# Cross attention and a 4-bit FFN on one core: the dequantisation is spread over the setup and the projections of the first chunk, with two pairs of PSUM banks

## The reference

```python
# cross attention: 16 heads, dk = 8, 4 superposed states
qh, kh, vh = (interfere(proj(t, W, b)) for ...)      # t = LN(x), ctx, ctx
# interfere(y) = y + 0.1 * amp * einsum('bhsdi,hij->bhsdj', y, interference)
scores = einsum('bhqdm,bhkdm->bhqkm', qh, kh) / sqrt(8)
x = x + (softmax(scores, over keys) applied to vh) @ Wo.T + bo
# FFN with 4-bit weights, 512 -> 2 x 1376 -> 512
W[i, j] = sc[g[i], j] * (wq[i, j] - (zq[g[i], j] + 1))
gate, up = split(LN(x) @ W_gu);  x = x + (silu(gate) * up) @ W_d
```

## Time and profile before

| | |
|---|---|
| median of three runs | 906.57 us |
| profiled execution | 906.32 us, its span 904.6 us |
| mean granted TensorE clock | 0.90 |
| PE busy | 772.6 us, 85% of the span |
| DVE busy | 510.2 us, 56% |
| ACT busy | 438.3 us, 48% |
| POOL busy | 326.8 us, 36% |
| chain that ended last | PE 67%, DVE 15%, ACT 8%, issue 6%, DMA 2% |

### The profile page before, as it was taken

The page is one execution under the profiler, slowest core; times in us unless marked ns, Lnnn a source line. Parts: engine busy times, 40 slices in busy tenths (PEclk is TensorE's granted clock), DMA queues, the critical chain, the costliest instruction groups (busy, mean ns, idle before and its releaser), DMA issues.

```text
span 904.6 us, 23874 instructions
## 1 busy us (share of the span) xinstructions
PE 772.6 (85%) x9953; PEld 562.3 (62%) x9953; DVE 510.2 (56%) x1013; ACT 438.3 (48%) x806; POOL 326.8 (36%) x290
## 2 busy tenths in 40 slices
PE   5306457766799999999999999999999999999898
PEld 5303323322278857876787778677857885787484
DVE  6987745554465646655574556456645663644421
ACT  1426355676365526662555455454635462655120
POOL 6732324555314530543064114412431352144220
PEclk9758655565599999999999999999999999999999
DMA  8900113222101011002100110011001100010000
GB/s 248 292 23 1 50 32 89 69 56 63 32 25 28 3 49 50 3 3 71 28 2 14 60 28 3 13 60 28 2 21 52 28 2 25 3 27 3 24 1 23
DMA packets 20702, 36.98 MB, mean 41 GB/s; under 512 B 3374, under 2 KB 7602, under 8 KB 20592
## 3 DMA queue, kind: packets, MB, share of 16 engines
q1 hardware_dynamic: 20604, 35.48, 13.5%
HBM read 26.56 MB, written 4.19 MB: 34 GB/s over the span
## 4 chain that ended last, share of the span: by engine, by line
PE 67%; DVE 15%; ACT 8%; issue 6%; DMA 2%; SPq 1%; DVEq 0%; ACTq 0%; POOL 0%
PE bank L511 16%; PE bank L526 13%; PE bank L482 9%; PE bank L492 9%; PE bank L644 4%; DVE nmf L1166 4%; PE bank L638 3%; PE bank L661 3%; ACT arena L849 3%; PE bank L619 2%; PE bank L459 2%; DVE arena L1094 2%; DMA arena<-in_L_xattn_Wo 2%; DVE arena L985 2%; PE bank L443 2%
## 5 line engine op out<-in xcount | busy, mean ns | idle before, releaser
L511 PE MATMUL bank<-arena,WGU 128*128 128x256 f16 (+1 forms) x2112 | 247.0, 274 | 1.4 <-DVE arena L709 1.4
L511 PEld LDWEIGHTS bank<-arena,WGU 128*128 128x128 f16 (+1 forms) x2112 | 206.2, 100 | 27.5 <-DVE arena L709 1.6
L1368 POOL TENSOR_TENSOR arena<-arena 128x512 f16<-128x512 f32 x128 | 147.0, 1173 | 190.5 <-ACT arena L856 190.5
L482 PE MATMUL bank<-arena,WT 128*128 128x256 f16 x768 | 91.3, 281 | 40.4 <-DVE arena L709 39.1
L526 PE MATMUL bank<-WD,arena 128*128 128x512 f16 (+1 forms) x528 | 121.1, 379 | 0.0
L849 ACT ACTIVATE arena<-bank,small 128x512 f32<-128x512 f32 x128 | 89.1, 776 | 58.3 <-PE bank L644 58.3
L1355 POOL TENSOR_TENSOR arena<-arena 128x512 f16<-128x512 f32 (+1 forms) x48 | 51.7, 1077 | 172.2 <-ACT arena L829 172.2
L482 PEld LDWEIGHTS bank<-arena,WT 128*128 128x128 f16 x768 | 76.9, 101 | 54.6 <-issue 43.1
L492 PE MATMUL bank<-WT,arena 128*128 128x512 f16 x384 | 88.0, 387 | 1.8 <-DVE arena L707 1.8
L526 PEld LDWEIGHTS bank<-WD,arena 128*128 128x128 f16 (+1 forms) x528 | 49.4, 98 | 53.2
L1166 DVE TENSOR_REDUCE nmf<-bank 128x8 f32<-128x512 f32 x128 | 79.4, 682 | 4.4 <-PE bank L619 4.2
(11 more groups left out here) (157 smaller groups left out, 1068.8 us busy)
## 6 DMA issues: line engine op xcount, KB each, us to landing
arena<-in_L_ffn_qweight_gu SPq DMA_DIRECT2D x8, 688.0 KB, 5.4
arena<-arena SPq DMA_DIRECT2D x32, 144.0 KB, 3.0
WT<-in_ctx SPq DMA_DIRECT2D x8, 512.0 KB, 15.1
arena<-in_ctx SPq DMA_DIRECT2D x8, 512.0 KB, 3.7
arena<-in_x SPq DMA_DIRECT2D x8, 512.0 KB, 3.6
out_y<-arena SPq DMA_DIRECT2D x16, 256.0 KB, 2.1
arena<-in_L_ffn_qweight_down SPq DMA_DIRECT2D x10, 256.0 KB, 3.4
arena<-in_L_xattn_Wk SPq DMA_DIRECT2D x1, 1024.0 KB, 6.6
```

The lines of the kernel that those rows point to most:

```text
L482: mm = e.matmul(jb[:, g2 * TOK:(g2 + 1) * TOK], WT[:, w, sp, kb, g * P:(g + 1) * P], src[:, mp, kb, :], start=(n == 0), stop=(n == 11))
L511: mm = e.matmul(pb[0:m, i * TOK:(i + 1) * TOK], WGU[:, sp, kb, half * INTER + fb * P:half * INTER + fb * P + m], x2T[:, mp, kb, :], start= ...
L1368: e.tensor_tensor(phl[:, a, 1, :], pring[:, a, :], phl[:, a, 0, :], ALU.subtract).then_inc(S["p_lo"], 1)
```

## The change

- **The ticks.** There are 40 now, from the ctx maxima on. Three stand in the setup (after the 4th, 6th and 8th ctx maximum), three after the scales, two after each of the first two weights' halves, five behind the first key operations and five behind the value rows; slots 0 and 1 have one each, every batch four, and the tail two. The steps of a tick are further apart: on TensorE unit n - 2, on VectorE the integers of n and the product of n - 3, on ScalarE the conversion of n first, then the scaled difference of n - 2 and the high half of n - 4, on POOL the remainder of n - 5.
- **The banks.** Units below 17 alternate between two pairs, the second being JB[0] and JB[1]. From unit 17 on there is the one pair, as before. The folds have the four AB banks for all weights.
- **The tables.** The gate/up scales are split in three parts on VectorE in a layout over 128 partitions, the zero points in one over 32, and 12 and 4 transfers bring them into the row layout. The one-hot matrix of gate/up is made on VectorE. The quantisation scales have an all-reduce of their own. The down tables stay on POOL and ScalarE.
- **The rest.** The 32 copies that permute Wo are on ScalarE. The quantised weights are loaded earlier. The transposed ctx is made ahead of the ticks of w0.

The diff, cut to its core:

```diff
-TICKS = ND + 3
-FIRST_SLOT = 2
-TICK_ENDS = [0] * FIRST_SLOT + [TICKS * (k + 1) // (SLICES - FIRST_SLOT) for k in range(SLICES - FIRST_SLOT)]
...
+TICKS = ND + 5
+PLACES = ["ctx4", "ctx6", "ctx8", "scales", "w0", "w1", "keys", "values"] + list(range(SLICES))
+TICKS_AT = {"ctx4": 1, "ctx6": 1, "ctx8": 1, "scales": 3, "w0": 2, "w1": 2, "keys": 5, "values": 5}
+BATCH_TICKS = [0, 1] + [slot[j] for slot in IN_BATCH for j in (0, 2, 3, 3)] + AT_TAIL[:2]
+assert sum(TICKS_AT.values()) + len(BATCH_TICKS) == TICKS
+TICKS_AT.update((k, BATCH_TICKS.count(k)) for k in BATCH_TICKS)
+TWO_PAIRS = sum(TICKS_AT[p] for p in PLACES[:PLACES.index("values") + 1]) - 3
+def ticks(place):
+    before = sum(TICKS_AT.get(p, 0) for p in PLACES[:PLACES.index(place)])
+    return range(before, before + TICKS_AT.get(place, 0))
 
...
+            load_w(e, 1)
+            e.dma_start(scw, sc_gu.rearrange("g (r n) -> (g r) n", r=32)).then_inc(S["scw_loaded"], 16)
+            e.dma_start(zraww[0:32, :], qz_gu.rearrange("g (r n) -> (g r) n", r=8)).then_inc(S["zw_loaded"], 16)
...
-                e.dma_start(scgu[32 * i:32 * i + GROUPS_GU, :], sc_gu).then_inc(S["sc_loaded"], 16)
                 e.dma_start(scd[32 * i:32 * i + GROUPS_D, :], sc_d).then_inc(S["sc_loaded"], 16)
-            for c in range(NCHUNK):
-                e.dma_start(cmax_st[:, c].rearrange("p (t n) -> p t n", t=TILES), c_d[c]).then_inc(S[f"ctxm_loaded{c}"], 16)
+            e.dma_start(gidx_d[0:96, :].bitcast(I32), gi_d.partition_broadcast(96)).then_inc(S["gid_loaded"], 16)
+            load_w(e, 2)
+            e.dma_start(gidx_gu[0:96, :].bitcast(I32), gi_gu.partition_broadcast(96)).then_inc(S["gi_loaded"], 16)
+            load_w(e, 0), load_w(e, 3)
+            for c in range(4):
+                load_ctx_max(e, c)
+            load_piece(e, 0)
+            e.wait_ge(S["sc_zeroed"], 2)
+            e.wait_ge(S["wide_ready"], 1)
+            for i in range(PARTS):
+                for g in range(GROUPS_GU):
+                    e.dma_start(sc3_gu[32 * i + g:32 * i + g + 1, :], sc3w[32 * g:32 * g + 32, i, :]).then_inc(S["sc_table"], 16)
+            e.wait_ge(S["zwide_ready"], 1)
+            for g in range(GROUPS_GU):
+                e.dma_start(z_gu[g:g + 1, :], zw[8 * g:8 * g + 8, :]).then_inc(S["z_table"], 16)
+            for c in range(4, NCHUNK):
+                load_ctx_max(e, c)
             e.dma_start(cin, c_d[0]).then_inc(S["ctx_loaded"], 16)
             e.dma_start(xin, x_d[0]).then_inc(S["x_loaded"], 16)
-            load_piece(e, 0)
             load_piece(e, 1)
             e.dma_start(bo_row[:, :], bo.partition_broadcast(P)).then_inc(S["bo_loaded"], 16)
+            for i in range(2, 6):
+                load_next_piece(e, i)
...
-                banks = bank[4 * (i % 2):4 * (i % 2) + 4]
                 e.wait_ge(S[f"w_loaded{w}"], 16)
...
+                if i:
+                    e.wait_ge(S["fold_evicted"], i)
+                else:
                     e.wait_ge(S["bias_evicted"], 1)
...
-                            mm = e.matmul(banks[cb][:, g * P:(g + 1) * P], wraw[w][:, g, cb * P:(cb + 1) * P],
...
+            for place in ("ctx4", "ctx6", "ctx8", "scales"):
+                pe_ticks(e, place)
+            e.wait_ge(S["fold_evicted"], 4)
+            for t in range(TILES):
+                pe_transpose_tile(e, -1, f"cT{t}", cin, S["ctx_loaded"], 16)
+            pe_ticks(e, "w0")
+            pe_ticks(e, "w1")
+        def pe_ticks(e, place):
+            for n in ticks(place):
+                pe_dequant(e, n - 2)
+        def dq_banks(n):
+            return (JB[0], JB[1]) if n < TWO_PAIRS and n % 2 == 0 else (GB, UB)
...
+            reached(e, S["d_w"], n - 1 if n < TWO_PAIRS else n)
+            e.matmul(scale[0:m, 0:cols], hot[0:64 + groups, pick], sc3[0:64 + groups, c0:c0 + cols], start=True, stop=True)
...
             if first:
+                pe_ticks(e, "keys")
                 e.wait_ge(S["wlo_done"], 2)
...
+                pe_ticks(e, "values")
...
                 e.wait_ge(S["wlo_done"], 3)
                 e.wait_ge(S["t_lo"], t_at(-1, "xT1"))
+                e.wait_ge(S["d_w"], TWO_PAIRS)
...
         def act_setup(e):
+            for i in range(2):
+                act_scale_part(e, i)
...
             for i, w in enumerate(WORDER):
+                if w == 3:
+                    act_permute(e)
...
-                    ins = e.activation(wraw[w][:, cb], bank[4 * (i % 2) + cb][:, :], ACT.Copy)
+                    ins = e.activation(wraw[w][:, cb], AB[cb][:, :], ACT.Copy)
...
+            act_scale_part(e, 2)
+            for place in ("ctx4", "ctx6", "ctx8", "scales"):
+                act_ticks(e, place)
             e.wait_ge(S["scale_ready"], 1)
             act_whi(e, 0)
             act_hi(e, -1, "cT0"), act_hi(e, -1, "cT1")
+            act_ticks(e, "w0")
             act_whi(e, 1)
+            act_ticks(e, "w1")
+        def act_permute(e):
+            e.wait_ge(S["w_loaded3"], 16)
...
+                            ins = e.activation(wop[g][:, at:at + 64].rearrange("p (i q d) -> p i q d", i=KB, q=2),
+                                               ap(wraw[3][:, g], 0, P, 64 * hh + 32 * a + j, [(128, KB), (2, 2), (4, 8)]), ACT.Copy)
+            ins.then_inc(S["wo_permuted"], 1)
+        def act_ticks(e, place):
+            for n in ticks(place):
+                act_dequant_conv(e, n)
+                act_dequant_scaled(e, n - 2)
+                act_dequant_hi(e, n - 4)
...
+            if n == 0:
+                e.wait_ge(S["scq_ready"], 1)
             e.wait_ge(S["d_gathered"], n + 1)
...
-            e.activation(dq[n % 4][0:m, 0:cols], GB[0:m, 0:cols], ACT.Copy,
-                         scale=SC[0:m, 6:7] if down else SC[0:m, 5:6]).then_inc(S["d_scaled"], 1)
-        def act_dequant(e, k):
-            act_dequant_scaled(e, k - 1)
-            act_dequant_hi(e, k - 2)
-            act_dequant_conv(e, k)
+            e.activation(dq[n % 4][0:m, 0:cols], dq_banks(n)[0][0:m, 0:cols], ACT.Copy,
+                         scale=SCQ[0:m, 1:2] if down else SCQ[0:m, 0:1]).then_inc(S["d_scaled"], 1)
...
             if first:
                 act_whi(e, 2)
+                act_ticks(e, "keys")
...
-                act_scale_part(e, 1)
                 act_v_hi(e, c)
+                act_ticks(e, "values")
...
             e.tensor_reduce(MX[:, 10:11], iv, AX_X, ALU.max, apply_absolute_value=True)
-            for i, w in enumerate(WORDER):
+            dve_tables(e)
+            dve_zeros_d(e)
...
-                if i == 3:
-                    for g in range(KB):
-                        for hh in range(2):
-                            for j in range(2):
-                                for a in range(2):
-                                    at = (4 * hh + 2 * j + a) * 64
...
+                if i == 0:
+                    dve_hot_gu(e)
...
+                if c in (3, 5):
+                    dve_ticks(e, f"ctx{c + 1}")
...
             e.tensor_reduce(MX[:, 4:5], MXC, AX_X, ALU.max).then_inc(S["max_ready"], 1)
+            dve_ticks(e, "ctx8")
...
+            dve_ticks(e, "scales")
             dve_wlo(e, 0)
             dve_lo(e, -1, "cT0"), dve_lo(e, -1, "cT1")
+            dve_ticks(e, "w0")
             dve_wlo(e, 1)
+            dve_ticks(e, "w1")
...
+            e.wait_ge(S["scw_loaded"], 16)
+            e.tensor_reduce(MXQ[:, 0:1], scw, AX_X, ALU.max, apply_absolute_value=True)
+            link(e, e.tensor_copy(sc3w[:, 0, :], scw))
+            link(e, e.tensor_tensor(restw, scw, sc3w[:, 0, :], ALU.subtract))
+            link(e, e.tensor_copy(sc3w[:, 1, :], restw))
+            e.tensor_tensor(sc3w[:, 2, :], restw, sc3w[:, 1, :], ALU.subtract).then_inc(S["wide_ready"], 1)
...
+            link(e, ins)
+            e.tensor_scalar(zw[0:32, :], zintw[0:32, :], -1.0, -1.0, ALU.mult, ALU.add).then_inc(S["zwide_ready"], 1)
+            e.wait_ge(S["sc_loaded"], 16 * PARTS)
+            e.tensor_reduce(MXQ[0:GROUPS_D, 1:2], scd[0:GROUPS_D, :], AX_X, ALU.max, apply_absolute_value=True).then_inc(S["maxq_ready"], 1)
+        def dve_hot_gu(e):
+            e.wait_ge(S["gi_loaded"], 16)
...
+            e.tensor_scalar(hot_gu[0:96, :], h, GM[0:96], None, ALU.is_equal).then_inc(S["hot_ready"], 1)
+            e.wait_ge(S["maxq_all"], 1)
...
+        def dve_ticks(e, place):
+            for n in ticks(place):
+                dve_dequant_int(e, n)
+                dve_dequant_w(e, n - 3)
...
             e.wait_ge(S["d_scaled"], n + 1)
-            e.tensor_tensor(w, w, UB[0:m, 0:cols], ALU.mult).then_inc(S["d_w"], 1)
+            e.tensor_tensor(w, w, dq_banks(n)[1][0:m, 0:cols], ALU.mult).then_inc(S["d_w"], 1)
...
-            e.memset(scd[0:96, :], 0.0)
-            e.memset(scgu[0:96, :], 0.0).then_inc(S["sc_zeroed"], 1)
-            pool_hot(e, GROUPS_D, INTER, gidx_d, hot_d)
-            pool_hot(e, GROUPS_GU, DM, gidx_gu, hot_gu)
...
```

(25 more changed lines are left out.)

199 lines of the change are left out of this document (103 added, 96 removed).

## The result

The changed kernel took 926.98 us (median of four, 926.07 to 927.94) against 905.84 us, a ratio of 1.0235 (95% interval 1.0215 to 1.0256). The forecast was 931 us. The profiled execution took 926.26 us with a span of 924.0 us. These rows are the busy time of the changed kernel cut at the landmarks of the forecast (width, busy us of PE, PEld, DVE, ACT and POOL, granted clock, share of DMA, GB/s); they answer to the earlier trace rows.

What follows compares the result with a forecast made beforehand. Before 240.3 us the dequantisation loop across TensorE, ScalarE and VectorE sets the pace; the rest stays. 906.3 + 4.2 (setup) + 40.3 (scales to scores) - 19.7 (batches and tail) = 931.1 us, range 914 to 946.

Steps and rivals of the forecast that it cites:

- Step 1: Setup up to the scales: they are ready at 64.1 us instead of 59.95, 4.2 us later.
- POOL's idle time: Setup: POOL's 7.14 us of idleness behind today's all-reduce moves along with the new small all-reduce at 13.7 us.
- the start of the folds: Setup: TensorE folds Wk only after POOL's operation, ScalarE's second part and the bias copies end at 24.2 us.
- the permutation: Setup: the 32 permuting copies of Wo on ScalarE take 6.4 to 9.0 us; 6.4 was taken.
- the second and third fold: Setup: after a first fold of 5.7 us, these TensorE folds take 3.2 us each, alternating with evictions.
- The rival in which the setup does not stall: Setup: POOL's 7.14 us don't follow the small all-reduce, 8.9 us less, 922 us; chance 0.2.
- Step 2: From the scales to the first scores: 89.2 us with nineteen ticks there, 40.3 us more than before.
- the rival that packs the ticks: Scales to scores: ScalarE alone sets the stretch, scores 58 us after the scales, 900 us; chance 0.1.
- Step 3: Four batches and tail: 27.7, 25.9, 28.2 and 30.0 us, sum 111.8, less than before by 19.7.
- The two causes: Batches: TensorE waits for VectorE in each slot, and ScalarE's conversion before scaling lengthens the loop from 3.19 to 3.8 us.
- The port rival: Ticks: VectorE and POOL block each other, 14 ticks wait 0.9 us more each, 12.6 us, 944 us; chance 0.13.
- a useless second pair: Ticks: the second pair of banks doesn't help, each tick costs 3.8 us, 26 more, 957 us; chance 0.04.

Runs made afterwards that it cites:

- the kernels with the biases first: Changed kernel with ScalarE copying the folded biases ahead of its second part of the down scales, 922.05 us; later kernels keep this edit.
- the kernel with the second part moved: Changed kernel with biases copied first and the second part of the down scales behind the first eviction on ScalarE: 917.32 us.

## Why the prediction was right

The mechanisms held, and the sizes were off by up to 5 us, in both directions. The total is closer than its terms: 3.5 us too little in the setup stand against 4.8, 3.0 and 1.2 us too much in the other stretches, and that they cancel in part is luck.

**Step 1** (forecast +4.2, measured +7.7). POOL's idle time (7.1 forecast, 7.90 measured), the start of the folds (24.2, 24.58) and the permutation (6.4, 6.51) are as forecast. The mis-sized term is that of the second and third fold: 3.2 us each were put down, and they took 3.81 and 5.44, the third of them at a mean granted clock of 0.70. That is 2.8 of the 3.6 us. The first fold's 5.7 us were right (5.91), but not for the reason given, the idle time ahead of it: with 0.85 us of idle time it took 5.2 to 6.6 us in the kernels with the biases first. On the copies the row of VectorE's own (0.20) gave the right sum, 6.51 us for 32 on ScalarE, and by luck: it is the length of one copy there, while on VectorE undisturbed ones follow each other in 0.12 us; on ScalarE one lasts 0.31 us and they follow each other in 0.20. The estimate from the Trainium skill (VectorE: DVE Perf Modes, The TRN2 errata), 7.7 us, was 1.2 too high. The rival in which the setup does not stall is excluded by POOL's 7.90 us in the changed kernel. Its price, 8.9 us, is close to what the kernel with the second part moved gave at the scales (8.7), but from other terms: the first fold started 8.5 us earlier there (6.7 forecast) and was 0.13 us shorter (2.2 forecast).

**Step 2** (forecast 89.2 from the scales to the scores, measured 84.4). By landmark the key projection was forecast at 25.0 and came at 22.4, the query projection at 70.7 and came at 66.7. The five ticks at the keys took 10.0 us and those at the values 9.1, as forecast (9.7 and 9.4). The time was gained ahead of them: the first weight half started at 5.7 us after the scales (6.7 forecast), the second was done at 17.7 (20.0), and the keys' ticks began at 34.1 (37.7). The groups did end or start on waits: seven waits of 2.7 to 5.6 us for VectorE or TensorE make 24.5 of ScalarE's 34.2 idle us. ScalarE was busy 50.2 of 84.4 us, and the rival that packs the ticks (scores at 58) fell.

**Step 3** (forecast 27.7, 25.9, 28.2 and 30.0; measured 26.6, 24.9, 28.2 and 29.1). The two causes were named and both are shown by the kernels that take them away one at a time: a unit in the one pair waits for VectorE in each slot (15 us for the lag), and the loop grew from 3.19 to 3.76 us (3 to 7.5 us for the order).

**The rivals.** The port rival put 12.6 us on VectorE's conversions. In the changed kernel, over the stretch from the scales to the scores (ns, least, median, most):

```profile
L1194 DVE TENSOR_SCALAR arena<-arena,smalli x19: 394/480/1394, 67.6 to 146.7; 128x512 uint32<-128x512 uint32 x13, 128x352 uint32<-128x352 uint32 x6
```

Most are undisturbed. The nineteen took 11.03 us together, where their usual lengths (0.48 and 0.40) make 8.6, so 12.6 us are not there. The blocking itself is real: it took 4.3 and 5.4 us in the kernel before, and some 14 from VectorE's copies (18.29 us, where at the pace of the last sixteen all would take 4). There POOL's operations are 3 to 5 us long; the remainders of the ticks take 1.2. For a useless second pair 26 us on top of the forecast were put down; the kernel with one pair took 26 more than the changed one.

## What to carry to other kernels

Work that is moved has a price at its new place and a credit at its old one, and the credit is not the work's length: here the batches kept their time although they lost 10 of their 22 ticks, because the longer lag and the new order, written for the two pairs at the new place, held in the batches too. Give each stretch the lag that its buffers allow: with the one pair of banks the longer lag made TensorE wait for a product that stands later in VectorE's queue. (No run tried the short lag with the two pairs.) A stall on one engine costs what stands behind it in the queue of whoever waits for it; moving one 0.6 us operation behind an eviction gave back 9.7 us, and moving it one step less far gave 4.9; some 2 us of what is missing are slower folds.
